# Q, K and V convolutions of an attention stage as 32x32 products on the normalised image, with the input product folded into their weights

## The reference

```
x = x + L0(gn(x))      # 3x3 convolution with products of pixel pairs
x = x + L1(gn(x))      # 3x3 convolution
x = x + L2(gn(x))      # attention of a convolutional LSTM cell
x = x + L3(gn(x))      # spectral convolution (Hartley transform)

# L2, x the normalised image
xin = W_in x + b_in                          # 1x1 product
q = conv(xin, Wq[0], 'SAME')                 # 4 heads x 8 channels x 1024 pixels
k = conv(xin, Wk[0], 'VALID')                # 4 heads x 8 channels x 900 pixels
v = conv(xin, Wv[0], 'VALID')
w = softmax(q^T k);  a = v w                 # per image and head
# the cell state is zero: the other three attentions are zero or need only
# the mean of v over the pixels; then gates, tanh and W_out
```

## Time and profile before

| what | value |
|---|---|
| median of 3 runs | 320.7 us (318.45 to 322.28) |
| profiled execution | 321.3 us, of it 319.5 us span in the trace |
| PE busy | 291.6 us, 91% of the span |
| DVE busy | 209.0 us, 65% |
| ACT busy | 183.5 us, 57% |
| POOL busy | 30.2 us, 9% |
| bytes moved | 15.28 MB, 48 GB/s on average |

### The profile page before, as it was taken

One profiled execution on the slowest core, in us unless ns is written; L12 is line 12 of the kernel. 1 busy time (PEld: TensorE's weight loads), 2 busy tenths in 40 slices (PEclk: granted clock), 3 DMA queues, 4 the chain that ended last, 5 costly groups with the idle time before them and its releaser, 6 DMA issues.

```text
span 319.5 us, 10019 instructions
## 1 busy us (share of the span) xinstructions
PE 291.6 (91%) x4308; PEld 130.8 (41%) x4316; DVE 209.0 (65%) x483; ACT 183.5 (57%) x346; POOL 30.2 (9%) x34
## 2 busy tenths in 40 slices
PE   5999999798998999999999999999999899877774
PEld 2686634233455334333333333343333232334751
DVE  5980272577368647886977888879788122477664
ACT  1102011116246898897988888878888898313700
POOL 6400000010000000100100101001010010800000
PEclk9999999999999999999999999999999999999799
DMA  7100000003671483794000000000000000000001
GB/s 224 72 4 4 4 12 0 2 0 89 198 139 32 105 141 88 185 330 167 1 2 4 3 4 2 2 5 3 4 2 2 2 3 2 0 2 3 2 4 66
DMA packets 3819, 15.28 MB, mean 48 GB/s; under 512 B 807, under 2 KB 1623, under 8 KB 3359
## 3 DMA queue, kind: packets, MB, share of 16 engines
q1 hardware_dynamic: 3519, 14.54, 16.6%
q0 software_dynamic: 256, 0.11, 0.2%
HBM read 12.17 MB, written 2.37 MB: 45 GB/s over the span
## 4 chain that ended last, share of the span: by engine, by line
PE 41%; DVE 12%; issue 5%; ACT 5%; DMA 2%; ACTq 0%; DVEq 0%
PE ps L1187 11%; PE ps L1137 10%; PE ps L1169 10%; PE ps L1307 3%; ACT arena_b L662 3%; DVE sums L870 3%; DVE mx L875 3%; PE ps L1193 2%; PE ps L1252 2%; DMA arena_a<-mt_sb 2%; ACT arena_a L691 1%; PE ps L1328 1%; DVE arena_b L965 1%; DVE arena_a L940 1%; PE ps L1260 1%
## 5 line engine op out<-in xcount | busy, mean ns | idle before, releaser
L662 ACT ACTIVATE arena_b<-ps 128x512 f32<-128x512 f32 x232 | 126.3, 616 | 20.8 <-PE ps L1169 19.6
L1137 PE MATMUL ps<-arena_a 72*32 72x450 bf16 (+1 forms) x889 | 88.5, 355 | 3.0 <-DVE mx L870 1.5
L1169 PE MATMUL ps<-arena_a 75*32 75x512 bf16 x896 | 85.1, 380 | 0.8 <-DMA arena_a<-mt_sb 0.5
L875 DVE TENSOR_REDUCE mx<-ps 128x1 f32<-128x450 f32 x120 | 68.7, 618 | 3.6 <-PE ps L1137 3.5
L870 DVE CUSTOM_DVE_ANT_0 sums<-ps,relus 128x450 bf16<-128x450 f32 x68 | 42.1, 625 | 29.1 <-PE ps L1137 26.4
L1187 PE MATMUL ps<-arena_b,vt 128*32 128x512 f32 x448 | 58.9, 596 | 1.4 <-ACT arena_b L662 1.0
L1137 PEld LDWEIGHTS ps<-arena_a 72*32 72x32 bf16 (+1 forms) x889 | 27.6, 96 | 55.0 <-DVE mx L875 20.0
L990 PE MATMUL ps<-zeros 128*128 128x512 bf16 (+1 forms) x149 | 39.0, 370 | 5.7 <-DMA xa<-x 3.5
L670 ACT ACTIVATE relus<-ps 128x450 f32<-128x450 f32 x68 | 38.8, 570 | 9.4 <-PE ps L1137 8.1
L1169 PEld LDWEIGHTS ps<-arena_a 75*32 75x32 bf16 x896 | 24.9, 96 | 36.6 <-issue 14.1
L1019 PE MATMUL ps<-arena_a,cst 32*32 32x512 f32 x720 | 26.0, 609 | 0.0
(11 more groups left out here) (130 smaller groups left out, 225.9 us busy)
## 6 DMA issues: line engine op xcount, KB each, us to landing
arena_b<-wmodes SPq DMA_DIRECT2D x1, 4096.0 KB, 20.5
arena_a<-k_scratch SPq DMA_DIRECT2D x9, 258.4 KB
arena_a<-q_scratch SPq DMA_DIRECT2D x12, 96.0 KB
arena_a<-q_scratch SPq DMA_DIRECT2D x3, 384.0 KB
k_scratch<-arena_b SPq DMA_DIRECT2D x3, 344.5 KB, 3.8
cst<-consts SPq DMA_DIRECT2D x1, 901.0 KB, 8.1
arena_a<-k_scratch SPq DMA_DIRECT2D x6, 129.2 KB
q_scratch<-arena_b SPq DMA_DIRECT2D x6, 128.0 KB, 5.0
```

What stands on the lines that cost most here:

```text
L662: nc.scalar.activation(probs[:, n % PRING, :], ps[:, SCORE_RING[n % len(SCORE_RING)], :], ACT.Exp).then_inc(expd, 1)
L875: nc.vector.tensor_reduce(mx[:, a, e:e + 1], bank, AX.X, ALU.max).then_inc(max_read, 1)
L1137: last = mm(ps[j:j + width, block_bank(i), 0:KHALF], qst[0:PAIR_ROWS, e, g, qt * P + j:qt * P + j + width], kst[0:PAIR_ROWS, g, at:at + KH ...
L1169: last = mm(ps[32 * j:32 * j + 32, bank, :], kst[0:S_ROWS, g, k0:k0 + 32], qst[0:S_ROWS, e, g, :], start=True, stop=True)
```

## The change

**Weights.** xin is no longer formed. Two products of 432 columns give the q, k and v weights with W_in folded in (`wcomb`), for four images at once, and nine of 96 columns give the bias of every tap (`biasw`). They stand on PE behind the first convolution stage, where 20 fillers were and now 11 are; ACT copies them to SBUF, and the first product of L1 (L1052 before, L1103 now) also waits for these copies. The constants for it, 2152 columns, come as one more transfer at the start.

**Convolutions.** `conv()` now makes 32x32 products from the padded normalised image: row group b is image b, column group j is one kind of result. It walks over 10 steps (the bias through a mask of valid taps, then 9 taps), in each over the images, and in each over the kinds. The first call makes q of the first half, both halves of k and the key difference (156 products, into banks 0 to 3, one bank per image); the second makes both halves of v and q of the second half (120 products, banks 4 to 7). DVE subtracts two row ranges of the image once for the key difference.

**Split.** ACT and DVE split one image after the other, four operations of 128x512 for q and all of k together. Its transfers have the 4 heads of an image outermost. K goes through SP, q of image 0 through ACT's queue, q of images 1 to 3 through POOL's. The second half of q is copied by ACT behind the first relu after the turn, split by four POOL operations behind the first turn's transfer, and then written and stacked by SP.

**V, means, ring.** V is copied by ACT and DVE to `vsb` and turned by 28 products of 64 rows, 128 weight columns and 32 moving columns, and 16 with 4 weight columns. They stand between the maxima blocks of image 0: two behind each of blocks 4 to 11, three behind each of blocks 20 to 29 (the last one alone). All write to bank 3; ACT copies them to `vt` and `vrest` behind the relus of blocks 16 and 32. The products of the mean of v stand behind blocks 35, 39 and 43. Blocks 0 to 45 and the turn use a ring of three banks (0, 1, 2); the filler stands ahead of each block, in the block's own bank and behind its wait. The order from the first score tile on is the same.

The diff, cut to its core:

```
+EARLY_RING = (0, 1, 2)
+SIDE_BANK = 3
+CONV_FIRST = (("q", 0), ("k", 0), ("k", 1), ("k", "diff"))
+CONV_SECOND = (("v", 0), ("v", 1), ("q", 1))
+TURNS_FIRST = 4
+TURNS_SECOND = 16
+MEANS_AT = (35, 39, 43)
...
-            ring = SCORE_RING + MAX_RING if i < prologue else MAX_RING
+            ring = EARLY_RING if i < early_blocks else MAX_RING
...
+            def write_k(b):
+                sp.wait_ge(split_l, b + 1)
+                for j, (kind, part) in enumerate(CONV_FIRST):
+                    if kind == "k":
+                        at = {0: 0, 1: KHALF, "diff": KDIFF}[part]
+                        sp.dma_start(k_dram[:, :, 4 * b:4 * b + 4, at:at + KHALF].rearrange("c t h n -> h c t n"),
+                                     parts[32 * j:32 * j + 32, b, :, 0:KHALF]).then_inc(kd_written[b], 16)
...
-            keep_clock(6, 13)
+            keep_clock(2, 11)
             pe.wait_ge(padded, 2)
+            pe.wait_ge(wc_ready, 3)
...
+                for step in range(10):
+                    for b in range(B):
+                        for j, (kind, e) in enumerate(tiles):
+                            dst = ps[32 * j:32 * j + 32, bank + b, 0:n].rearrange(
+                                "p (y x) -> p y x", x=W if kind == "q" else KH)
...
+                                last = mm(dst, wcomb[rows, KINDS[kind], step - 1, :], conv_rows(image, kind, e, u, v),
+                                          start=(step == 1 and e == "diff"), stop=(step == 9), skip_group_check=True)
+                last.then_inc(conv_done, 1)
...
+                if i < early_blocks:
+                    keep_clock(block_bank(i), 1, 256)
...
-            pe.wait_ge(q_part[2], 2)
-            keep_clock(2, 6)
+            pe.wait_ge(split_r, B)
+            keep_clock(0, 2)
             pe.wait_ge(k_in[0], PARTS * 16)
-            keep_clock(2, 5)
+            keep_clock(0, 2)
             pe.wait_ge(q_in[0], PARTS * 16)
-            pe.wait_ge(vt_ready, 2 + HEADS)
...
                     max_block(*item[1:])
-                    if item[1] < prologue:
-                        keep_clock(O_RING[0], 1, 256)
+                    i = item[1]
+                    if TURNS_FIRST <= i and first_turns:
...
+                        last = [turn_values(first_turns.pop(0)) for _ in range(2)][-1]
...
+                    if i in MEANS_AT:
+                        means(MEANS_AT.index(i))
```

More of the change, by code:

```diff
@@ L234 @@
     N_CONST += _n
+N_ALL = N_CONST
+for _name, _n in [("win4", P), ("qkvw", 3 * 9 * 32), ("binbase", 8 + P), ("qmask", HW)]:
+    CONSTS[_name] = (N_ALL, _n)
+    N_ALL += _n
+PAST_MAPS = 15040
+assert PAST_MAPS >= N_MAPS * NP and PAST_MAPS + N_ALL - N_CONST <= 8192 + G * KW // 2
 def build(nc, x, consts, wmodes, max_rows, out):
@@ L370, in build @@
         gb_ready = sem("gb_ready")
-        qd_written = [sem("qd_written0"), sem("qd_written1")]
-        kd_written = sem("kd_written")
+        qd_written = [sem(f"qd_written{b}") for b in range(B)]
+        q1_written = sem("q1_written")
+        kpad_written = sem("kpad_written")
+        kd_written = [sem(f"kd_written{b}") for b in range(B)]
         ones_in = sem("ones_in")
@@ new lines, in means @@
+            def means(step):
+                images = [slice(32 * b, 32 * b + 32) for b in range(B)]
+                if step == 0:
+                    pe.wait_ge(vt_ready, 2 + HEADS)
+                    pe.wait_ge(win_ready, 6)
+                    mm(ps[:, SIDE_BANK, 16:25], c_("win"), win9[:, 0, :], start=True, stop=True).then_inc(win_done, 1)
+                elif step == 1:
+                    pe.wait_ge(win_scaled, 1)
+                    v2w = c_("v2w").rearrange("p (s o) -> p s o", o=32)
+                    for r in images:
+                        for s in range(9):
+                            last = mm(ps[r, SIDE_BANK, 0:1], v2w[r, s, :], win9[r, 1, s:s + 1], start=(s == 0), stop=(s == 8))
+                    last.then_inc(a2_done, 1)
+                else:
+                    pe.wait_ge(a2_ready, 1)
+                    proj2 = c_("proj2").rearrange("p (s o) -> p s o", o=32)
+                    for r in images:
+                        for i in range(3):
+                            last = mm(ps[r, SIDE_BANK, 8 + i:9 + i], proj2[r, i, :], a2[r, :], start=True, stop=True)
+                    last.then_inc(gb_done, 1)
@@ L1181, in values @@
                 bank = O_RING[half % len(O_RING)]
+                if t == 0 and half == 0:
+                    pe.wait_ge(q1_copied, 1)
+                    pe.wait_ge(vt_ready, 2 + HEADS)
                 if t == 0 and half >= len(O_RING):
```

450 lines of the change are left out of this document (236 added, 214 removed).

## The result

The changed kernel takes 363.0 us (361.5 to 414.8, four runs), the kernel before 320.1 us; the ratio is 1.132, with an interval of 1.122 to 1.142. The sign was forecast, the size not: 339 us, with 347 as upper end.

The account below looks back on a forecast made before the run. The end of PE's row was taken to decide most stages. 321.3 - 4.5 (first block) + 1 (clock) + 14.9 (maxima) + 7.0 (turn to score) = 339.7, less 0.6 for the profiled run: 339 us, range 325 to 347.

Parts of the forecast that it names:

- The planes: Weight and bias products plus eleven fillers run from 43.0 to 49.0 us, making the planes some 1.0 us late.
- the second call: Second call of the new convolutions: 20 q passes per tile at 0.447 us, 8.9 us, ending at 79.6 us.
- the ring: Maxima of image 0: three banks close a loop of 1.96 us over two pairs, 0.98 a pair where 0.60 stood.
- a block with two turns: Maxima of image 0: block and filler 0.305 us, two turns 0.44, gaps 0.30 from changing between bf16 and fp32.
- Rival C: Convolutions: only one image's four tiles run at a time, 59 us instead of 18, about 380 us; chance 0.03.
- A: Maxima stay at DVE's pace, pairs at 0.60 us, only the transfers gain: about 315 us; chance 0.06.
- B: Turns of V hide in the ring's waits, pairs take 0.98 us: about 322 us, no change; chance 0.08.
- The clock term: PE idle ahead of the first maxima block lowers the clock: 1 us for slow first blocks, between 0 and 2.
- The loads: Key loads of image 0, ahead of the first maxima block, land 3.0 to 5.2 us after being issued.
- -4.5 us: First maxima block at 86.5 us against 91.05, late planes included; ends -8.2 and -3.
- The writes' shape: K writes with 4 heads outermost use a quarter of the transfer engines, 80 GB/s; image 0's k and q take 4.5 us.
- After the first score: From the first score tile on both kernels have the same order, so the same length was expected.

Follow-up runs that it names:

- the best version: New convolutions with the maxima of before, wide writes of k, V gathered to 128 rows and turned densely, 28 fillers; ratio 1.011 to the kernel before.
- the ring of three banks with the early copy: Changed kernel with V turned densely ahead of the first block, 52 fillers, q's second-half copy moved to DVE ahead of that block; 339.5 us (1.062).

## Why the prediction was wrong, step by step

**What held.** The path was read rightly: most of the time was lost in the maxima of image 0 (27.2 us over the kernel before) and behind the turn (10.2 us), little ahead of them (2.8 us). The planes start at 48.20 us (49.0 forecast), the second call takes 8.5 us (8.9), a split 2.7 us (2.9), the ring takes 1.88 us for two pairs (1.96), a block with two turns at full clock 0.97 us (1.045). That the writes land at 83.2 us (82.5) is in part luck: the split ended 1.8 us later than forecast, and the writes took 1.1 us less. Rival C fell: 312 passes in 10.3 us at 1.00 are 0.033 us a pass, so the tiles run together, four kinds on one row group included. The rule of the Trainium skill that weight loads are pulled ahead where their row groups don't conflict ("TensorE: Matmul & The Clock Gate", "Part 3: Packing small matmuls — row/col tiling") would have warned of this order; the trace shows at most the step from 0.0297 us to 0.033. Rivals A and B fell too: pairs are 0.94 us apart where they have no turns and the clock is full (A wanted under 0.75), and a visit of two turns adds 0.67 us to the 0.305 of block and filler (B wanted under 0.2).

**The clock term, "1 us, between 0 and 2", is the step that failed.** I took the low clock for the end of an idle stretch that a few blocks make good. The runs show three things in its place. First, idle PE lowers it (the changed kernel, in the 11 us before its keys), but work as sparse as this change puts on PE lowers it with PE busy all the time: 28 thin products in the kernel before cost 19 us up to the first score tile, 28 dense ones 6. Second, once at 0.50 it stays there through blocks and fillers that hold 1.00 when they are entered at 1.00: 20 us in the kernel before without its fillers, with no turns between the blocks. In these traces it rose among the score tiles (at 157 us in the changed kernel) or behind runs of fillers with nothing between, as here at the turn of the changed kernel:

```profile
130.09 2.77 PE L1033 MATMUL ps<-zeros 128*128 128x512 bf16 x6
```

Third, the change makes three such places in a row (wait for the keys, turns between blocks, means between blocks), so that the clock is below full speed from 84 to 158 us but for a few us at the turn. In the maxima of image 0, eight visits with two turns at 1.70 us in place of 1.045 give 5.2 us, four with three at 2.12 (116.53 to 118.65 us and three like it) in place of 1.265 give 3.4, six with small turns (6.2 us in place of 5.0) 1.2, fourteen blocks without turns at 0.59 us 1.4: 11.2 of the 12.3 us by which the stretch exceeds the forecast without its clock term (39.4 against 27.1). Between turn and score, the means alone add 1.3 of the 3.2 us.

**The loads, "3.0 to 5.2 us", were mis-sized.** They take 9.6 us, and 8 alone. The upper end was the distance from the *last* issue of the kernel before to its first block, which is no measure of a transfer: from its first key load at 82.45 us to the block at 91.05 were 8.6 us, and of these the fillers ahead of the block held a part. In the kernel before without fillers the loads had landed at most 7.2 us after their first issue (81.30 to 88.45 us). This term is 5.6 us of the first stretch's 7.3; fillers between the landing and the block are another 1.0, the writes 0.7.

**"-4.5 us" was a gain in no version.** The kernel before convolved k first, and its ACT began to copy it, in its trace, at:

```profile
72.21 0.55 ACT L635 ACTIVATE arena_b<-ps 128x450 f32<-128x450 f32 x1 [4.83 <-PE ps L1084]
```

The new first call ends at 72.6 us, so the first result is no earlier; what the change saves lies in q and v. The loads of image 0 are issued at 82.45 us in the kernel before, at 83.18 in the changed one, and no sooner than 81.4 in any version with the new convolutions. I weighed the whole row of convolutions (25.1 us) against two calls and said that only the way to the first block matters, but did not ask when the old k was ready. I also read the fillers from 88.03 us as PE waiting for the stacked queries. That was wrong: without these fillers the first block comes at 88.45 us, released by DVE's last copy of V (the row in the experiments), so the queries were there by then, and the 91.05 us that I counted from was set by the fillers themselves. The first call itself, 11.9 us where 9.3 were forecast, ran at 0.69 and 0.89 in its first two windows, another dip; at 1.00 it takes 10.3.

**The writes' shape was sized well, and is worth little.** Four heads outermost and 32 rows outermost, in the same window of the changed kernel and of the one with wide writes and the maxima of before, PE's windows with DMA share and GB/s:

```profile
76.00:80.00 4.00, 4.00 (x127) 1.00 0.22 57
```

```profile
76.00:80.00 4.00, 4.00 (x127) 1.00 0.68 139
```

0.22 is near a quarter of the engines. This agrees with the rule of the Trainium skill ("DMA: Bandwidth & Descriptors", "Why a DMA increments its semaphore by 16 and not by 1") that the outermost sizes of both sides set the number of engines. But the writes land only 1.8 us sooner; issuing the six instructions alone takes 4.4 to 4.9 us with four heads outermost and 3.9 to 4.8 with 32 rows.

**After the first score** the stretch is 1.3 us longer, and the clock is low until 158 us; q of the second half did not show up as a wait. Why the fold of the weights starts a dip in some kernels only, and why fillers in front of it did not remove it, stays open, and so does how much of the loss of the best version (1.011) lies there.

## What to carry to other kernels

Thin products (here fp32, of 32 moving columns or of one), set between dense ones, can cost the clock for tens of us even where PE never waits: use a dense form (128 rows a transpose), keep them among dense work as the kernel before did, and price such a step at half clock when judging it. Faster work on an engine pays only if the first consumer's first operand comes out earlier; compare the time of the first result, not the length of the stage, and measure a transfer from its own issue, not from that of the last one in the queue. A row of fillers up to the first consumer hides what it waits for: take the fillers out once before reading that wait. Where two changes come together, as the new convolutions and the new order here, try them apart: the convolutions with the maxima of before lost 1 to 6% in every version, the whole change 13%.

## What the hardware showed that was not expected

The granted clock fell from 1.00 to 0.60 and 0.50 with PE busy for 4.00 of 4.00 us (the kernel before with 28 thin products, from 97 us on), while 28 products of 512 columns in the same places kept 1.00. Once low, it stayed at 0.50 from 89 to 109 us through 32 blocks and fillers with PE busy all the time (the kernel before without fillers), which run at 1.00 in the kernel before, and it rose behind the run of fillers at the turn. Around the 36 products of one column of the mean, 2.13 us, it went to 0.81 and then 0.50 where they stand between blocks (the ring of three banks with the early copy), and stayed at 1.00 where they stand between convolutions (the kernel before).
